# A segmented linear-memory scan: the memory update in one round, and q's feature on VectorE

## What is computed

```python
def elu1(x): return jax.nn.elu(x) + 1.0           # exp(x) for x < 0, x + 1 above

def step(carry, inp):                             # one segment of 32 tokens
    mem, z = carry
    q_s, k_s, v_s, qn_s, kn_s = inp               # with and without rotation
    scores = jnp.where(mask, einsum('bhnd,bhmd->bhnm', q_s, k_s) * SCALE, -inf)
    sdpa = einsum('bhnm,bhmd->bhnd', softmax(scores), v_s)
    sq, sk = elu1(qn_s), elu1(kn_s)
    mem_out = einsum('bhnk,bhkv->bhnv', sq, mem) / (sq . z + 1e-6)
    out = beta * mem_out + (1.0 - beta) * sdpa
    prev_v = einsum('bhnk,bhkv->bhnv', sk, mem) / (sk . z)
    mem = mem + einsum('bhnk,bhnv->bhkv', sk, v_s - prev_v)
    z = z + sk.sum(axis=2)
    return (mem, z), out
```

## Time and profile before

| | us |
|---|---|
| median of 3 runs | 3374.51 |
| lowest, highest | 3370.74, 3388.3 |
| the profiled execution | 3378.05 |
| its span | 3376.2 |
| the scan in it | 1903 to 3376 |

### The profile page before, as it was taken

How to read it: one execution, slowest core, us unless ns; L and a number is a source line. 1 busy time by engine, 2 the same in 40 slices (tenths; PEclk the granted TensorE clock), 3 DMA queues, 4 the chain that set the end, 5 groups by cost and what they waited for, 6 DMA issues and landing times. The chain is left out here.

```text
span 3376.2 us, 133974 instructions
## 1 busy us (share of the span) xinstructions
PE 2890.8 (86%) x56049; PEld 1694.1 (50%) x56049; DVE 2501.5 (74%) x7471; ACT 1930.5 (57%) x3909; POOL 1697.3 (50%) x1600
## 2 busy tenths in 40 slices
PE   5675999999999999997233299999999999999998
PEld 2332333333333333336222167676677767676776
DVE  4567788887888888866660678788888788787876
ACT  4564778787787878772000155555555555555553
POOL 4663000000000000003016499999999999898996
PEclk9777899999999999998565599999999999999999
DMA  3467333333233333309201200000000000000000
GB/s 123 169 207 231 70 83 85 89 77 87 75 85 84 87 87 76 87 25 286 82 27 29 74 4 11 11 11 11 11 11 11 11 11 11 10 7 9 11 7 11
DMA packets 179424, 210.31 MB, mean 62 GB/s; under 512 B 28608, under 2 KB 140288, under 8 KB 178560
## 3 DMA queue, kind: packets, MB, share of 16 engines
q1 hardware_dynamic: 176256, 200.31, 21.3%
q0 software_dynamic: 2560, 1.35, 0.4%
HBM read 125.17 MB, written 75.63 MB: 59 GB/s over the span
## 5 line engine op out<-in xcount | busy, mean ns | idle before, releaser
L778 ACT ACTIVATE at_pA<-at_ps 128x512 f32<-128x512 f32 x1024 | 569.1, 608 | 131.6 <-DVE at_ps L831 131.1
L840 DVE CUSTOM_DVE_ANT_0 at_junk<-at_ps,w_cmask 128x512 f32<-128x512 f32 (+3 forms) x1024 | 462.7, 488 | 169.9 <-PE at_ps L682 169.9
L658 POOL CAST at_mrow<-at_neg 16x128 bf16<-16x128 f32 x64 | 18.0, 282 | 1110.3 <-DVE at_neg L803 1110.3
L831 DVE TENSOR_TENSOR at_ps<-at_ps,w_ratio 128x128 f32<-128x128 f32 (+3 forms) x1024 | 490.4, 493 | 67.2 <-PE at_ps L676 67.0
L784 ACT ACTIVATE at_pB<-at_ps 128x512 f32<-128x512 f32 (+1 forms) x768 | 395.9, 538 | 77.3 <-PE at_ps L692 76.8
L2099 ACT ACTIVATE sc_ee<-sc_ps 128x512 f32<-128x512 f32 x256 | 153.0, 598 | 497.9 <-PE sc_ps L1955 496.5
L676 PE MATMUL at_ps<-at_aq,at_ak 72*128 72x512 bf16 x1024 | 355.9, 391 | 3.5 <-DMA at_ak<-parts_scratch 3.1
L1919 POOL TENSOR_TENSOR sc_rb<-sc_rb,v_sin 128x512 f32<-128x512 f32 x256 | 327.0, 1278 | 48.5 <-DVE sc_ra L2143 48.1
L682 PE MATMUL at_ps<-at_bk,at_bq 72*128 72x512 bf16 (+3 forms) x1024 | 273.2, 309 | 52.3 <-DMA at_bk<-parts_scratch 31.6
L1955 PE MATMUL sc_ps<-sc_xT,v_wqkv 128*128 128x512 f32 x512 | 293.1, 655 | 18.8 <-DVE sc_ra L2143 16.6
L689 PE MATMUL at_ps<-at_bq,at_bk 75*128 75x512 bf16 (+3 forms) x1024 | 283.3, 303 | 18.3 <-DVE at_mx L840 17.3
(11 more groups left out here) (315 smaller groups left out, 6377.9 us busy)
## 6 DMA issues: line engine op xcount, KB each, us to landing
parts_scratch<-fr_parts SPq DMA_DIRECT2D x64, 384.0 KB, 4.1
at_bq<-parts_scratch SPq DMA_DIRECT2D x192, 96.0 KB
at_bk<-parts_scratch SPq DMA_DIRECT2D x192, 96.0 KB
at_aq<-parts_scratch SPq DMA_DIRECT2D x192, 96.0 KB
at_ak<-parts_scratch SPq DMA_DIRECT2D x192, 96.0 KB
v_scratch<-fr_v SPq DMA_DIRECT2D x32, 352.0 KB, 4.3
at_v<-v_scratch SPq DMA_DIRECT2D x32, 352.0 KB, 3.5
parts_scratch<-fr_parts SPq DMA_DIRECT2D x32, 256.0 KB, 3.9
```

Source lines behind the costliest of these rows:

```text
L778: act.activation(pA[:, n % A_RING, j * S:(j + 1) * S], src, ACT.Exp).then_inc(exped, 1)
L831: dve.tensor_tensor(src[:, 0:wide], src[:, 0:wide], W["ratio"][:, S - wide:S], ALU.mult).then_inc(tilted, 1)
L840: ins = dve.tensor_tensor_reduce(junk[:, P * j * (j + 1) // 2:P * (j + 1) * (j + 2) // 2], src[:, col:col + wide], W["cmask"][:, S - wide: ...
```

## The change

**The update in one round.** `update` on TensorE now runs all four f at once, f into bank 2 + f, with f as the inner loop in place of hh, and stands behind `turn_heads`; the round between `turn_keys` and the output projection is gone. It gives one increment of `up`, for which both additions of VectorE wait, each then reading two banks. As it also writes banks 2 and 3, it waits for VectorE to have read the recalls (`qd`) and the scores (`sx`), and the recall of k in the next step waits for the first addition (`mu`). On VectorE the first addition moves behind the rotation of k.

**q's feature.** For q ScalarE leaves out relu(x). The new operation on VectorE (`sigma_q`) computes max(x + 1, exp(-relu(-x))) from the bank of q, which is the same function. It stands behind the rotation of q, and its semaphore `sgq` frees q's bank and releases the recall with q. GpSimd keeps k's feature alone (`sigma_k`). The rotation of q waits for one relu in place of two.

```diff
             for s in range(STEPS):
                 if s < PT:
-                    user(("q", s), "rp", 2 * s + 1)
+                    user(("q", s), "sgq", s + 1)
...
-                    def update(p, fs):
+                    def update(p, s):
+                        wait(pe, "ud", p + 1)
+                        wait(pe, "skc", p + 1)
+                        wait(pe, "qd", min(s - 1, PT))
+                        wait(pe, "sx", min(s, PT))
+                        wait(pe, "mu", 2 * p)
                         for g in range(BG):
-                            for f in fs:
-                                for hh in range(2):
-                                    ins = pe.matmul(ps[64 * hh:64 * hh + 64, 4 + f % 2, g * VE:(g + 1) * VE],
+                            for hh in range(2):
+                                for f in range(B1):
+                                    ins = pe.matmul(ps[64 * hh:64 * hh + 64, 2 + f, g * VE:(g + 1) * VE],
                                                     skN[32 * f:32 * f + 32, p % 4, g, 64 * hh:64 * hh + 64],
                                                     uu[32 * f:32 * f + 32, p % PAIRS, g, hh, :], start=True, stop=True)
                         ins.then_inc(G["up"], 1)
...
-                            wait(pe, "mu", 2 * (p - PAIRS + 1))
+                            wait(pe, "mu", 2 * (p - 2) + 1)
                             recall(p, 1, "kr_s")
...
                         p = s - 3
-                        if inside(p):
-                            wait(pe, "ud", p + 1)
-                            wait(pe, "skc", p + 1)
-                            wait(pe, "sx", min(s, PT))
-                            wait(pe, "mu", 2 * p)
-                            update(p, (0, 1))
                         if inside(s - 4):
                             project_out(s - 4, (2, 3))
                         if inside(p):
                             turn_heads(p, s)
-                            wait(pe, "mu", 2 * p + 1)
-                            update(p, (2, 3))
+                            update(p, s)
...
-                        act.activation(ee[:, n % 2], x, ACT.Relu, scale=-1.0)
-                        act.activation(relu[:, n % 2], x, ACT.Relu).then_inc(G["ex"], 1)
+                        ins = act.activation(ee[:, which], x, ACT.Relu, scale=-1.0)
+                        if which == 1:
+                            ins = act.activation(relu[:], x, ACT.Relu)
+                        ins.then_inc(G["ex"], 1)
...
+                    def sigma_q(p):
+                        wait(dve, "mn", 2 * p + 1)
+                        wait(dve, "qr_s", p - 3)
+
+                        dve.scalar_tensor_tensor(sig[0][:, p % 4], ps[:, bank_of("q", p), :], 1.0, ee[:, 0], ALU.add, ALU.max).then_inc(G["sgq"], 1)
...
+                        if s < PT:
+                            rope(2 * s + 1)
                         p = s - 3
                         if inside(p):
                             update(p, 0)
-                        if s < PT:
-                            rope(2 * s + 1)
```

More of the change, by code:

```diff
@@ L1707, in scan @@
         ol = sb("ol", [P, 4, BG, 2, DH])
-        ee, relu = sb("ee", [P, 2, S]), sb("relu", [P, 2, S])
+        ee, relu = sb("ee", [P, 2, S]), sb("relu", [P, S])
         ra, rb = sb("ra", [P, 2, S]), sb("rb", [P, 2, S])
@@ L1717, in scan @@
         ps = ctx.enter_context(nc.psum_tensor("sc_ps", [P, 8, 512], F32))
[L1720 removed]
+        names = ("h_in0 h_in1 stat fact shift_d xn_d tq_d xnn_d xq_d step xt xt_c xqt xqt_c hb_d ffn ffn_c vp v_c pj ex mn rp sn sgq sgk add_d sS skt skc "
                  "sx se pt pvd old kr_s qr_s kd ud qd od up mu ott otc oproj ydone stored0 stored1").split()
@@ L1908, in _, with sigma_k @@
                 def _(pool):
-                    def sigma(n):
-                        p, which = divmod(n, 2)
-                        wait(pool, "mn", n + 1)
+                    def sigma_k(p):
+                        wait(pool, "mn", 2 * p + 2)
                         wait(pool, "qr_s", p - 3)
                         wait(pool, "skt", p - 3)
-                        pool.tensor_tensor(sig[which][:, p % 4], ee[:, n % 2], relu[:, n % 2], ALU.add).then_inc(G["sg"], 1)
+                        pool.tensor_tensor(sig[1][:, p % 4], ee[:, 1], relu[:], ALU.add).then_inc(G["sgk"], 1)
                     def rotate(n):
@@ L2012, in turn_keys @@
                     def turn_keys(p):
-                        wait(pe, "sg", 2 * p + 2)
+                        wait(pe, "sgk", p + 1)
                         wait(pe, "old", p)
@@ L2061, in _ @@
                         if inside(p):
+                            wait(pe, "sgq", p + 1)
                             wait(pe, "kd", p + 1)
@@ L2095, in features @@
                     def features(n):
-                        x = ps[:, bank_of("qk"[n % 2], n // 2), :]
+                        p, which = divmod(n, 2)
+                        x = ps[:, bank_of("qk"[which], p), :]
                         wait(act, "pj", n + 1)
-                        wait(act, "sg", n - 1)
-                        act.activation(ee[:, n % 2], x, ACT.Relu, scale=-1.0)
-                        act.activation(relu[:, n % 2], x, ACT.Relu).then_inc(G["ex"], 1)
+                        wait(act, ("sgq", "sgk")[which], p)
+                        ins = act.activation(ee[:, which], x, ACT.Relu, scale=-1.0)
+                        if which == 1:
+                            ins = act.activation(relu[:], x, ACT.Relu)
+                        ins.then_inc(G["ex"], 1)
                         wait(act, "ex", n + 1)
-                        act.activation(ee[:, n % 2], ee[:, n % 2], ACT.Exp, scale=-1.0).then_inc(G["mn"], 1)
+                        act.activation(ee[:, which], ee[:, which], ACT.Exp, scale=-1.0).then_inc(G["mn"], 1)
                     for s in range(STEPS):
@@ L2107, in _ @@
                             wait(act, "vp", s + 1)
-                            wait(act, "up", 2 * (s - PAIRS + 1))
+                            wait(act, "up", s - PAIRS + 1)
                             act.copy(uu[:, s % PAIRS, :, :, 0:DH], ps[:, bank_of("v", s), :].rearrange("p (g h d) -> p g h d", h=2, d=DH)).then_inc(G["v_c"], 1)
@@ L2120, in _ @@
                             wait(act, "skt", p + 1)
-                            wait(act, "up", 2 * (p - 3))
+                            wait(act, "up", p - 3)
                             act.copy(skN[:, p % 4].rearrange("p g r -> p (g r)"), ps[:, 6, :]).then_inc(G["skc"], 1)
@@ L2150, in update @@
                     def update(p, k):
-                        wait(dve, "up", 2 * p + k + 1)
+                        wait(dve, "up", p + 1)
                         m = V["mem"][:, p % PAIRS].rearrange("p (g f) v -> p f g v", f=B1)[:, 2 * k:2 * k + 2]
-                        dve.tensor_tensor(m, m, ps[:, 4:6, 0:BG * VE].rearrange("p b (g v) -> p b g v", g=BG), ALU.add).then_inc(G["mu"], 1)
+                        dve.tensor_tensor(m, m, ps[:, 2 + 2 * k:4 + 2 * k, 0:BG * VE].rearrange("p b (g v) -> p b g v", g=BG), ALU.add).then_inc(G["mu"], 1)
                     for s in range(STEPS):
```

5 lines of the change are left out of this document (2 added, 3 removed).

## The result

| | before | after |
|---|---|---|
| median, us | 3375.67 | 3459.99 |
| lowest to highest | 3370.74 to 3388.3 | 3453.0 to 3461.46 |
| span of the profiled execution | 3376.2 | 3457.5 |

The ratio is 1.0244, 95% interval 1.0224 to 1.0265: slower by 84 us, where I had predicted +11 with a range up to 3424. The prediction was wrong.

The account below looks back on a forecast made before the run. The prediction took TensorE's 10.49 us step, nothing in it waiting for GpSimd, as the bound, with gaps and stalls on top. Its terms, -15 + 22 + 0 - 5 + 9 = +11 us, gave 3385 us, range 3358 to 3424.

Parts of the forecast that it names:

- What bounds the kernel: Scan step: TensorE's rows without idle bracket cost 10.49 us; the mean 11.2 adds instruction-stream gaps and a stall per eight steps.
- Part 1: First update round leaves before the head transposes: 3.79 us stay, TensorE idles 0.7 per step, gaps give back -15 us.
- Part 2: Update as one burst of 64 instructions behind the head transposes: 0.86 us where a round of 0.69 stood, +22 us.
- rival 3: Update burst: four row groups above the same column groups overlap no better than two, 1.10 us; +41 us, 3415; chance 0.18.
- rival 2: Update burst runs at the pace of the tiles, 0.69 us; -11 us, 3363; chance 0.12.
- Part 3: q's feature on VectorE: 0.66 us more in its queue per step, off the path, 0 us.
- Part 4: VectorE's memory additions wait for the one burst, second ends 0.7 us later; plain step 0, fp8 rounding -5, y +9.
- (a): Rounding to fp8 on VectorE, k projection waiting for q's bank: 1.36 - 1.0 - 0.7 = -0.35, x 14 = -5 us.
- (b): Result y on VectorE frees the next v projection's bank 0.7 us later, without slack: +9 us.
- rival 4: VectorE becomes the bound, late at the k recall; each 0.3 us late is 38 us, +49, 3423; chance 0.08.
- the extreme of 3: Update burst: a column group takes one row group at a time, 1.91 us; +156 us, beyond 3500; chance 0.03.
- S: Theory from the experiments, not the prediction: TensorE can't have an instruction block sooner than about every 3.9 us on average.

Follow-up runs that it names:

- few recalls: Each recall as 8 products of 260 columns, not 32 of 65: kernel before 3349.49 us, kernel after 3353.23, two rounds with q's feature on VectorE 3294.41.
- mask edit: Mask products of the scores as 2 full matmuls, not 8: kernel before 3355.05 us (0.9945); with q's feature also on VectorE 3354.80 (0.9943).

## Why the prediction was wrong, by its own steps

**What bounds the kernel.** Wrong by what it left out. I read a step of 10.49 us without idle brackets and took it for the bound, and the gaps for noise on top. The mean step was 11.21, and outside the waits a block of instructions took 3.91 us, close to the figure of the kernels whose stream is overloaded. The gaps were the sign of a second bound just above the first.

**Part 1, the failing step: what the pause does to the gaps.** The path was right: pause, copy, 0.10 us, 3.79 us. Even the -15 us stood where I put it: over 120 steps of the trace after and 124 before, the mean from k projection to head transposes went from 3.99 to 3.88, -0.11 x 128 = -14. But I gave the pause only gaps to swallow. The gaps of the k recall (L1969 `sc_sk`, 3.1 to 30.1 us in the window), of the local product (0.9 to 17.4) and of the scores (9.0 to 15.5) grew from 13 us in 116 steps to 63 in 109, which is 0.47 per step and 60 us in the scan. Nearly all the loss stands in the stretch from q to k projection, which went from 5.90 to 6.50 us. I had put this effect at 0 to -19 us with no term for new gaps elsewhere; the runs showed +60. My reading, from the constant 3.90: what TensorE lost in the pause it would have had to make up at a higher pace, and the stream doesn't deliver at a higher pace. That is argued; what the transfers show is that these gaps wait for a block of instructions.

**Part 2, mis-sized.** The burst takes 0.91, not 0.86: +0.22 x 128 = 28 us in place of 22, between forecast and rival 3. Eight rows on each of eight tiles don't run at the pace of four tiles, as the earlier trace rows would allow, and no two row groups share a bank here. The Trainium skill (TensorE: Matmul & The Clock Gate, Part 3) says that a weight load overlaps with running matmuls only when the row group differs. By that the new order should be faster than the old one; the trace shows no difference, 0.91 and 0.92. But rival 2 took neighbours to be always in different row groups, and the two rows of one fp32 product lie in the same one in either order, so it was no clean test of the rule.

**Part 3, right.** q's feature on VectorE is 0, by its own run (0.9998).

**Part 4, right in its parts.** (a) The fp8 operations (L1549 to L1551) took 957 + 427 + 692 ns after, 487 + 1380 + 1605 before: 1.4 us less each time, where I had 1.7, and the wait of the k projection for the bank of q went from 14.1 to 6.4 us in the window, -8 per scan; I had -5. (b) The v projection waits for y for 9.0 us in the window, 0.083 per step, 11 in the scan; I had 9. No row has the k recall waiting for the memory add, so rival 4 is out.

**The sum.** -14 + 28 - 8 + 11 is +17 by the measured terms, near my +11; the gaps outside the pause's own stretch add 60, which makes +77 of the 84, and 7 us I didn't take apart. By the same terms the stream's part, gaps less what the pause took back, is 60 - 14 = 46 us. No rival named the stream: I had counted the idle rows of release "issue" as something that a wait can only absorb. Two slips in the prediction's figures change nothing: -18 and +51 on the median of 3374.5 are 3356.5 and 3425.5, where I wrote 3358 and 3424, and the chances of rivals 3 and 4 add up to 0.29 with the extreme of 3 (0.26 without it), not 0.28.

**What stays open.** Why a pause isn't used to load ahead. S says that the next block is only fetched as the present one is used. The transfers fit that wherever there is a gap, since the next one never starts until 1.05 us after it; whether it is so at every block, no run here shows. The nearly constant 3.90 is what the 13 kernels without the few recalls have in common (3.83 to 3.92, with those not in the table and with the waits for VectorE's read counted as waits), not a mechanism. Nor is 3.9 a floor for each block: a step holds 2.84 blocks (329 in 116 steps), and single steps like the earlier trace rows ran at 10.49 / 2.84 = 3.7. The mask edit gave 16 to 19 us where 23 would follow.

## What to carry to other kernels

Where TensorE works with many small tiles, count its instructions: divide the time of a stretch, less its waits, by the packets of the instruction queue, and compare that with a version that issues one burst twice. If that version moves no more blocks per microsecond, the stream is the bound: here a pause then cost time even though TensorE had less work, and leaving out instructions gave more than their own time. Gaps inside a burst that wait for no engine are no noise to be absorbed by idle time elsewhere; look whether each ends at a fixed time after a transfer of instructions. And an order without a wait in it is worth more than one with a shorter path, since a moved burst leaves its old place to whatever is released last there. Where a wait has several semaphores, check the engine that the profile names against the code: here it named the copy, and VectorE's read was the one.

## What the hardware showed unexpectedly

The instruction stream of TensorE has a rate that a kernel of 712 rows in 11.2 us all but reaches: 3.75 to 3.90 us for a block of 16 KB. In the traces before and after each gap inside a burst ends 1.2 to 1.6 us after such a block has landed. TensorE fell to 1.2 GHz for some microseconds after a wait of 2.02 us in one kernel and after a gap of 1.15 us in another, with granted clocks of 0.97 and 0.96 in their windows; the kernel after, with waits and gaps of up to 1.3 us, stayed at 1.00, so the length of one idle stretch alone doesn't tell. Eight tiles of 32x64 with a bank for each row group need 0.91 us for 64 rows of products, whichever of row group and column group changes first.
